# Sorting 2 x 262144 keys on one core: VectorE comparisons over the whole tile instead of over halves

## The reference

```
h = relu(layernorm(x)); x = x + L0(h)    # 4 steps: per edge type a linear map, sum over edges src -> dst, a GRU cell
h = relu(layernorm(x)); x = x + L1(h)    # graph attention
h = relu(layernorm(x)); x = x + L2(h)    # plain sum over edges
h = relu(layernorm(x)); x = x + L3(h)    # per source node: sum, max, mean of the edge features, then a perceptron
```

## Time and profile before

| | us |
|---|---|
| median of 3 executions | 7775.96 |
| lowest, highest | 7770.57, 7781.72 |
| the profiled execution's own time | 7751.51 |
| its span on the core | 7749.70 |

### The profile page before, as it was taken

The page is one execution under the profiler, slowest core; times in us unless marked ns, Lnnn a source line. Parts: engine busy times, 40 slices in busy tenths (PEclk is TensorE's granted clock), DMA queues, the critical chain, the costliest instruction groups (busy, mean ns, idle before and its releaser), DMA issues. The chain is left out here.

```text
span 7749.7 us, 95170 instructions
## 1 busy us (share of the span) xinstructions
PE 4891.3 (63%) x39275; PEld 2487.4 (32%) x39275; DVE 5101.1 (66%) x7708; ACT 1287.6 (17%) x2022; POOL 4049.8 (52%) x3297
## 2 busy tenths in 40 slices
PE   0110157534333334898988998979899647676678
PEld 0110123322112222455544555545555401111123
DVE  9889977534333343676756776657666489999700
ACT  0000012211111110000000000000000157777500
POOL 0027788888888884487872688836883000000130
PEclk9555578767666666999999999989999767667699
DMA  9910046533333337566664666646666143333398
GB/s 413 429 24 0 0 179 255 204 132 140 136 136 128 127 136 150 170 218 206 213 200 151 222 221 204 223 128 235 201 210 216 27 167 150 150 149 152 123 417 363
DMA packets 344776, 1414.97 MB, mean 183 GB/s; under 512 B 129310, under 2 KB 182836, under 8 KB 314516
## 3 DMA queue, kind: packets, MB, share of 16 engines
q1 hardware_dynamic: 159676, 1138.67, 39.3%
q10 hardware_dynamic: 79672, 239.96, 8.7%
q0 software_dynamic: 104992, 30.24, 3.2%
HBM read 1008.21 MB, written 400.36 MB: 182 GB/s over the span
## 5 line engine op out<-in xcount | busy, mean ns | idle before, releaser
L529 PE MATMUL ps_all<-ring,T 128*64 128x448 f16 x32928 | 3318.7, 364 | 1257.4 <-DVE T L1000 1246.7
L529 PEld LDWEIGHTS ps_all<-ring,T 128*64 128x64 bf16 x32928 | 1895.8, 113 | 2662.8 <-DVE T L1000 1280.2
L380 POOL DMA_INDIRECT mat_d<-cT,idxT x1563 | 1966.9, 1258 | 964.9 <-ACT cT L624 488.7
L424 POOL DMA_INDIRECT R<-in_edge_attr,eid x1568 | 1904.7, 1215 | 650.6 <-issue 476.9
L984 DVE TENSOR_SCALAR ring<-ring 128x3136 uint16<-128x3136 uint16 x812 | 803.3, 989 | 1003.3 <-DMA ring<-mat_d 956.1
L985 DVE TENSOR_SCALAR ring<-ring 128x3136 uint16<-128x3136 uint16 x812 | 786.3, 968 | 0.0
L1571 POOL DMA_INDIRECT sg<-seg_d,endI x49 | 57.3, 1170 | 1208.7 <-POOLq L163 1194.0
L483 PE MATMUL ps_all<-ident,R 128*128 128x128 f32 x448 | 108.3, 422 | 810.0 <-DVE R L754 810.0
L678 ACT ACTIVATE R<-R 128x1568 f32<-128x1568 uint16 x196 | 296.1, 1511 | 1749.8 <-DVE R L1021 1519.6
L1514 PE MATMUL ps_all<-ad,ones 3*128 3x384 bf16 (+1 forms) x686 | 321.6, 469 | 342.1 <-ACT ps_all L1484 341.2
L697 ACT ACTIVATE G<-ps_all 64x448 f32<-64x448 f32 x28 | 12.5, 541 | 2855.9 <-PE ps_all L529 2855.9
(11 more groups left out here) (371 smaller groups left out, 3393.5 us busy)
## 6 DMA issues: line engine op xcount, KB each, us to landing
ring<-mat_d SPq DMA_DIRECT2D x784, 784.0 KB
C<-csum_d SPq DMA_DIRECT2D x98, 3136.0 KB, 10.8
mat_d<-ring SPq DMA_DIRECT2D x98, 1568.0 KB, 39.7
csum_d<-R ACTq DMA_DIRECT2D x196, 784.0 KB
seg_d<-R ACTq DMA_DIRECT2D x32, 1568.0 KB, 7.1
msg_d<-t ACTq DMA_DIRECT2D x196, 128.0 KB
R<-in_edge_attr,eid POOLq DMA_INDIRECT x1568
mat_d<-cT,idxT POOLq DMA_INDIRECT x1563
```

Of the source, the lines that this page charges most:

```text
L380: pool.indirect_dma_start(mat_d, bass.IndirectOffsetOnAxis(idxT[:, col:col + 1], 0), cT[:, col:col + 1], None).then_inc(s_sc[g % 8], 16)
L424: pool.indirect_dma_start(slab[n % 2][:, c, 0:FA], None, attr, bass.IndirectOffsetOnAxis(eid[:, at:at + 1], 0)).then_inc(s_at[n % 2], 16)
L529: mm = pe.matmul(accs[h * D:(h + 1) * D, j, 0:GW], lhsT, ring[:, n % 6, h * HQ + j * GW:h * HQ + (j + 1) * GW], start=first, stop=True, sk ...
```

## The change

Within one layout a comparison now takes the whole tile: `plain(WHOLE, j)` is two instructions of 1024 outputs, and `ready` waits for the later of the two halves, which is the comparison just before it. `opening` does the same (four instructions of 512 outputs instead of eight of 256; at level 10 four of 512 as before). `whole_stage` becomes `plain(WHOLE, 10)`, with one wait instead of two. Halves remain in the last two distances in front of a turn and in `from_psum`. The order of the comparisons and what is computed stay the same.

```diff
+WHOLE = 2
+
 def in_turn(js):
-    body, tail = js[:-2], js[-2:]
-    return [(h, j) for j in body for h in range(2)] + [(h, j) for h in range(2) for j in tail]
+    return [(WHOLE, j) for j in js[:-2]] + [(h, j) for h in range(2) for j in js[-2:]]
+
+def halves_of(h):
+    return range(2) if h == WHOLE else (h,)
...
                     def half(buf, h):
-                        return Xb[buf][:, h * 1024:(h + 1) * 1024]
+                        return Xb[buf] if h == WHOLE else Xb[buf][:, h * 1024:(h + 1) * 1024]
...
                     def ready(h):
-                        if at[h]:
-                            dve.wait_ge(s_cx[n], at[h])
+                        last = max(at[k] for k in halves_of(h))
+                        if last:
+                            dve.wait_ge(s_cx[n], last)

                     def plain(h, j):
-                        a, b = (half(k, h).rearrange("p (o t d) -> p o t d", t=2, d=1 << j) for k in (cur[h], 1 - cur[h]))
+                        now = cur[halves_of(h)[0]]
+                        a, b = (half(k, h).rearrange("p (o t d) -> p o t d", t=2, d=1 << j) for k in (now, 1 - now))
                         ready(h)
                         dve.tensor_tensor(b[:, :, 0, :], a[:, :, 0, :], a[:, :, 1, :], ALU.min)
-                        ended(dve.tensor_tensor(b[:, :, 1, :], a[:, :, 0, :], a[:, :, 1, :], ALU.max), [h])
+                        ended(dve.tensor_tensor(b[:, :, 1, :], a[:, :, 0, :], a[:, :, 1, :], ALU.max), h)

-                    def opening(h, k):
+                    def opening(k):
...
+                        a, b = (Xb[z].rearrange("p (o s t d) -> p o s t d", s=2, t=2, d=1 << (k - 1)) for z in (cur[0], 1 - cur[0]))
+                        ready(WHOLE)
+                        for s in range(2):
+                            p, q = a[:, :, s, 1 - s, :], a[:, :, s, s, :]
+                            dve.scalar_tensor_tensor(b[:, :, s, 0, :], p, -1.0, q, ALU.mult, ALU.min)
+                            mx = dve.scalar_tensor_tensor(b[:, :, s, 1, :], p, -1.0, q, ALU.mult, ALU.max)
+                        ended(mx, WHOLE)
...
                     for k in range(1, 11):
-                        for h in range(2):
-                            opening(h, k)
+                        opening(k)
                         for j in range(k - 2, -1, -1):
-                            for h in range(2):
-                                plain(h, j)
+                            plain(WHOLE, j)
...
                         for h in range(2):
                             from_psum(t, h)
                         for j in range(k - 13, -1, -1):
-                            for h in range(2):
-                                plain(h, j)
-                        whole_stage()
+                            plain(WHOLE, j)
+                        plain(WHOLE, 10)
                         for h, j in in_turn([9, 8, 7]):
                             plain(h, j)
-                        for h, j in in_turn([6, 5, 4, 3, 2, 1, 0]):
-                            if j == 6:
-                                from_psum(t + 1, h)
-                            else:
-                                plain(h, j)
+                        for h in range(2):
+                            from_psum(t + 1, h)
+                        for h, j in in_turn([5, 4, 3, 2, 1, 0]):
+                            plain(h, j)
```

More of the change, by code:

```diff
@@ L122, in run @@
             n += 1
[L123 to L127, removed]
-        for h in range(2):
-            at[h], cur[h] = n, 1 - cur[h]
+            for k in halves_of(h):
+                at[k], cur[k] = n, 1 - cur[k]
     for k in range(1, 11):
-        run([(h, j) for j in range(k) for h in range(2)])
-    both()
-    both()
+        run([(WHOLE, j) for j in range(k)])
+    run([(WHOLE, 10)] * 2)
     run(in_turn([9, 8, 7, 6, 5, 4, 3, 2, 1, 0]))
@@ L136, in handed_over @@
         found.append([(at[h], cur[h]) for h in range(2)])
-        run([(h, j) for j in range(k - 11) for h in range(2)])
-        both()
+        run([(0, 6), (1, 6)] + [(WHOLE, j) for j in range(k - 12)] + [(WHOLE, 10)])
         run(in_turn([9, 8, 7]))
         found.append([(at[h], cur[h]) for h in range(2)])
-        run(in_turn([6, 5, 4, 3, 2, 1, 0]))
+        run([(0, 6), (1, 6)] + in_turn([5, 4, 3, 2, 1, 0]))
     assert cur[0] == cur[1]
@@ L741, in ended @@
                         ins.then_inc(s_cx[n], 1)
-                        for h in halves:
+                        for h in halves_of(halves):
                             at[h], cur[h] = done, 1 - cur[h]
                     def ready(h):
-                        if at[h]:
-                            dve.wait_ge(s_cx[n], at[h])
+                        last = max(at[k] for k in halves_of(h))
+                        if last:
+                            dve.wait_ge(s_cx[n], last)
                     def plain(h, j):
-                        a, b = (half(k, h).rearrange("p (o t d) -> p o t d", t=2, d=1 << j) for k in (cur[h], 1 - cur[h]))
+                        now = cur[halves_of(h)[0]]
@@ L772, in whole_stage @@
-                    def whole_stage():
-                        for h in range(2):
[L774 to L777, removed]
+                        ended(dve.tensor_tensor(b[:, :, 1, :], a[:, :, 0, :], a[:, :, 1, :], ALU.max), h)
@@ L790, in from_psum @@
                             ended(dve.scalar_tensor_tensor(b[:, :, 1, 1, :], v[:, :, 1, 0, :], -1.0, y[:, :, 1, :], ALU.mult,
-                                                           ALU.max), [h])
+                                                           ALU.max), h)
                         else:
@@ L795, in from_psum @@
                             dve.tensor_tensor(b[:, :, 0, :], v[:, :, 0, :], y, ALU.min)
-                            ended(dve.tensor_tensor(b[:, :, 1, :], v[:, :, 0, :], y, ALU.max), [h])
+                            ended(dve.tensor_tensor(b[:, :, 1, :], v[:, :, 0, :], y, ALU.max), h)
                     for k in range(1, 11):
-                        for h in range(2):
-                            opening(h, k)
+                        opening(k)
                         for j in range(k - 2, -1, -1):
-                            for h in range(2):
-                                plain(h, j)
+                            plain(WHOLE, j)
+                    ready(WHOLE)
                     for h in range(2):
-                        ready(h)
                         mv = dve.tensor_scalar(half(1 - cur[h], h), half(cur[h], h), sgn[:, h:h + 1], None, ALU.mult)
-                    ended(mv, (0, 1))
-                    whole_stage()
+                    ended(mv, WHOLE)
+                    plain(WHOLE, 10)
                     for h, j in in_turn([9, 8, 7, 6, 5, 4, 3, 2, 1, 0]):
```

## The result

The changed kernel takes 7822.57 us (median of 6, 7809.94 to 7834.29) against 7776.02 of the kernel before (median of 6, 7762.22 to 7795.29): 46.5 us more. The ratio is 1.0056, 95% interval 1.0040 to 1.0073. The forecast was 7831, +55.

A forecast was written before the change was run, and what follows sets the result against it. POOL's scatter stream was taken to bound the kernel until the last scatter. Second sort: 60 - 12 + 4 + 4 = +56, taken as +55; DVE -0.2; 7776 + 55 = 7831 us, range 7794 to 7866.

The forecast's parts named there:

- What bounds the kernel: From first to last scatter POOL's stream of 1563 scatters sets the end; DVE's second-sort time is not on it.
- DVE's own terms: Both sorts: a whole comparison goes from 2.41 to 2.40 us; the exposed first-sort part sums to -0.2 us.
- the part of the first sort that counts: Levels 12 to 18 of the first sort, exposed ahead of the first scatter; forecast -0.2 us, bounds +0.2 to -0.6.
- The cycle of three scatters in two comparisons: Second sort: every third scatter misses the gap and is held, three per 4.80 us instead of 3.80; +55 us.
- the endless row that I multiplied: Second sort: 117 whole comparisons reckoned as one continuous cycle, 47.5 scatters later, 60 us.
- the other losses: Second sort: about 4 us at today's rate elsewhere, and about 4 for finding the halves' beat after 14 rows.
- Downstream: After the second sort: the last scatter's delay moves everything later with it, the shift taken whole.
- The rivals: Alternatives to the forecast: no change 0.16, one scatter per whole comparison 0.07, faster 0.04.
- the scatters find the gaps after all: Second sort: DVE yields, a comparison grows to 2.52 us, the beat locks; 7776 within 5; no change 0.16.
- One scatter per comparison: Second sort: the hit at 1.10 fails, +122 to +134, about 7900 us; chance 0.07.
- Faster: Waits cost nothing in rows of whole comparisons and both sorts are exposed: 31 us less, 7745; chance 0.04.
- What was to be seen: Profile signs: one in three scatters about 1.96 us, mean near 1.2, some 295 in the second sort, earlier SP waits.

The follow-up runs named there:

- Run 5: Kernel before, with step 0's three adds per row block cut into pieces of 1024 columns; 7502.83 against 7777.43 us, ratio 0.9653.
- Run 1: Whole-tile comparisons in the first sort only, second sort in halves as in the kernel before; 7770.71 against 7777.43 us, ratio 0.9993.
- run 2: Whole-tile comparisons in the second sort only, first sort in halves as in the kernel before; 7821.1 against 7777.43 us, ratio 1.0061.
- run 6: Kernel before, with step 0's adds cut into pieces of 896 columns; 7549.3 against 7776.45 us, ratio 0.9701.
- run 3: Changed kernel, each whole comparison of the second sort issued as four instructions of 512 outputs; 7774.89 against the kernel before's 7777.43 us, ratio 0.9997.
- run 4: Changed kernel, a one-column memset after each whole comparison of the second sort; 7766.22 against the kernel before's 7776.45 us, ratio 0.9985.

## Why the prediction was right, by its own steps

- **What bounds the kernel.** Right. Run 5 is the strongest evidence: nothing changed but that DVE's adds are more and narrower instructions, in a stretch where DVE has time to spare; over the whole stream the mean scatter fell from 1258 to 1078 ns, 1563 x 0.180 = 281 us, and the kernel's time by 275.
- **DVE's own terms.** Right: 2.41 and 2.39 us for a comparison. Run 1 shows no cost in the first sort (0.9983 to 1.0002). The forecast of -0.2 us for the part of the first sort that counts agrees with the traces. It can be measured from DVE's first comparison after the first turn to the sort's last instruction. That is 278.81 us in the kernel before (the earlier trace rows and the first line below) and 278.24 in run 1 (the other two).

```profile
494.66 0.69 DVE L754 TENSOR_TENSOR R<-R 128x512 f32<-128x512 f32 x1
```

```profile
216.36 0.61 DVE L820 TENSOR_TENSOR R<-ps_all,R 128x256 f32<-128x256 f32 x1 [25.49 <-ACT R L642]
494.60 0.69 DVE L800 TENSOR_TENSOR R<-R 128x512 f32<-128x512 f32 x1
```

In the four profiles whose first sort works in halves (the kernel before, runs 2, 5 and 6) it is 278.76 to 278.90, in the four that take the whole tile there (the changed kernel, runs 1, 3 and 4) 278.24 to 278.87: in the mean 0.25 us less. By the rule of the Trainium skill that I weighed ("VectorE: DVE Perf Modes", "Rules for kernel authors": count instructions, not semaphores) it should have been 6.7 us less. Run 1's time alone would not decide this, as its interval of -13 to +2 us around -5 holds both; the traces do, and so do the distances in them (1.25 behind a wait, 1.14 without). So it is not the first sort that puts run 1 some 5 us (if it is there at all) and run 4 some 10 us under the kernel before; what does stays open.

- **The cycle of three scatters in two comparisons.** Right, seen as drawn. Its size was +50 us in the sort (62 - 12) where I summed +56 and took +55: the long holds make 56 x 1.0 = 56 us where the endless row that I multiplied gave 60, since in a row with an odd number of comparisons the last one has no miss, and the other losses come to 6 where I took 8. (I took these from 14 rows; the sort has 24 rows of whole comparisons, ten of them before the first turn.)
- **Downstream.** Right that nothing is made up after the last scatter: 46.2 us there, 46.5 at the end. Not quite right before it. I took the shift whole, as POOL has only bare issue between its scatters from 1490 to 2957 us. But POOL can also make time up by being held less, and it did: over all 1563 scatters its busy time grows by 45 us (1966.9 to 2012.2), while in the sort alone, up to 1024 us, it lost 51 more than before, so that some 6 us came back behind the sort. The forecast of +55 took about 5 us too much in the sort and missed these. The two profiled executions differ by 60.1 us at the end of the span; the 14 us more arise after the last scatter, and single executions of one kernel differ by as much (7762.22 to 7795.29).
- **The rivals.** That the scatters find the gaps after all does not happen by itself, but run 4 shows how near it was: at 2.53 instead of 2.40 us per comparison nearly all do. One scatter per comparison was not seen. Faster was not either, since POOL is held.
- **What was to be seen.** Last instruction of the second sort 11.4 us earlier (1023.14 to 1011.75; 10 to 15 said), SP's waits for POOL before 1480 us 69.3 instead of 7.4, mean scatter 1.17 (1.2 said), 301 scatters up to 1008 us (295 said for the whole sort, which ends at 1012).

## What to carry to other kernels

A wide DVE instruction can cost POOL's indirect DMAs more than it costs DVE. Here comparisons and adds with two inputs held scatters, and so did uint16 conversions with one. If POOL's stream is the path, count which DVE instructions run beside it and how long each bars the way, also where DVE's own time is free. Two regular streams meet by their beat, so compare the distance between gaps with the other stream's cadence, and not only the widths; here 2 x 0.60 + 0.06 and 2.53 fit 1.26, and 2.40 does not, and narrower pieces can be worse (896 columns against 1024). And a merge of instructions pays its fixed costs back only if no wait on the immediate predecessor takes their place.

## What the runs showed of the hardware that was not expected

- A scatter that arrives within about 0.02 us after the start of a DVE instruction of 512 outputs mostly gets in, and DVE is put back 0.06: in the kernel before's second sort 179 of 187 do. At 0.10 it is held until about 1.10 us into an instruction of 1024 outputs. In the changed kernel the ten that come up to 0.03 after the start of one of 1024 outputs all get in, and the two at 0.05 are held. The Trainium skill, in "GPSIMD Engine Reference", section "Key points", names the shared interface; the trace agrees, and gives the price, which goes up to nearly the whole DVE instruction for one indirect DMA (1.00 of 1.14 us here, 3.06 us beside adds of 3.43 at 1978.32 us in the kernel before).
- On two of the chips the kernel before took 25% longer (9744.13 and 9716.17 against 7777.43 us). In the profiles of other variants there, instructions came late on PE and DVE while POOL scattered; the cause is not known.
